# A fused group-norm, pair-mix and blur kernel on one core: wave 0 transposed as loaded, wave 1's statistics on ScalarE, filter and x1 statistics reordered

## What is computed

```python
def pair_mix(p, Wa, ba, Wb, bb, Wg, bg, Wo, bo):      # p (2, 64, 64, 64)
    a = p @ Wa + ba
    b = p @ Wb + bb
    g = sigmoid(p @ Wg + bg)
    ab = einsum('bijk,bikl->bijl', a, b)
    return g * ab @ Wo + bo

def gn(v): # 32 groups of 2 channels, each less its mean, over sqrt(variance + 1e-5)

x = x + pair_mix(gn(x), Wa, ba, Wb, bb, Wg, bg, Wo, bo)
x = x + depthwise_conv(gn(x), filt)   # 4x4 taps on a zero-stuffed map: 2x2 taps per output
```

## Time and profile before

| | us |
|---|---|
| median of 3 runs (lowest to highest) | 62.74 (62.19 to 62.99) |
| the profiled execution | 62.93 |
| its span | 61.0 |
| busy in the span: PE, DVE, POOL, ACT | 48.2, 41.5, 38.0, 29.3 |

### The profile page before, as it was taken

The page is one execution under the profiler, slowest core; times in us unless marked ns, Lnnn a source line. Parts: engine busy times, 40 slices in busy tenths (PEclk is TensorE's granted clock), DMA queues, the critical chain, the costliest instruction groups (busy, mean ns, idle before and its releaser), DMA issues.

```text
span 61.0 us, 2458 instructions
## 1 busy us (share of the span) xinstructions
PE 48.2 (79%) x1038; PEld 36.6 (60%) x1038; DVE 41.5 (68%) x111; ACT 29.3 (48%) x56; POOL 38.0 (62%) x51
## 2 busy tenths in 40 slices
PE   3999989998997985979999976998789899940000
PEld 3998878664865964756986735975468756400000
DVE  1073578888865679627479895479879978999200
ACT  5400005124494140784339999248892708990000
POOL 1000035809999599997281876984882997899500
PEclk9999999999999999999999999999999999999755
DMA  0899993000000000000000004031004004000494
GB/s 0 215 326 307 322 393 134 0 11 0 0 11 0 0 11 0 0 0 16 0 0 11 0 0 172 11 119 63 0 5 172 8 3 172 5 0 0 172 350 165
DMA packets 2604, 4.84 MB, mean 79 GB/s; under 512 B 289, under 2 KB 417, under 8 KB 2593
## 3 DMA queue, kind: packets, MB, share of 16 engines
q1 hardware_dynamic: 2592, 4.69, 22.4%
HBM read 2.59 MB, written 2.10 MB: 77 GB/s over the span
## 4 chain that ended last, share of the span: by engine, by line
PE 32%; POOL 24%; DVE 10%; issue 8%; ACT 4%; POOLq 2%; DVEq 0%
POOL y L253 11%; PE ps_ot L608 6%; PE ps_ab L641 6%; POOL rstd L218 6%; PE ps_ag L629 5%; POOL gn L240 5%; PE ps_ot L681 4%; PE ps_ag L653 2%; DVE y L468 2%; DVE bsb L445 2%; ACT gate L315 2%; PE ps_ab L665 2%; POOLq L55 2%; DVE part L414 2%; ACT rt L302 2%
## 5 line engine op out<-in xcount | busy, mean ns | idle before, releaser
L253 POOL TENSOR_TENSOR y<-y,prod 128x512 f32<-128x512 f32 x11 | 14.0, 1273 | 5.0 <-DVE y L468 4.6
L218 POOL TENSOR_TENSOR rstd<-veps,half 128x2 f32<-128x2 f32 (+1 forms) x7 | 5.7, 819 | 11.1 <-DVE veps L438 11.1
L583 PE MATMUL ps_ab<-zeros 128*128 128x128 f32 x54 | 9.3, 337 | 1.0 <-DVE zeros L486 1.0
L247 POOL TENSOR_TENSOR xb<-xs,par 128x512 f32<-128x512 f32 x8 | 8.5, 1098 | 1.6 <-issue 1.6
L583 PEld LDWEIGHTS ps_ab<-zeros 128*128 128x128 f32 x54 | 8.5, 244 | 1.0 <-DVE zeros L486 1.0
L315 ACT ACTIVATE gate<-ps_ag,par 128x512 f32<-128x512 f32 x8 | 5.5, 687 | 7.4 <-PE ps_ag L653 7.4
L302 ACT ACTIVATE rt<-ps_ot 128x512 f32<-128x512 f32 x7 | 4.0, 593 | 10.0 <-PE ps_ot L608 10.0
L345 ACT ACTIVATE prod<-x,coef 128x512 f32<-128x512 f32 x11 | 7.6, 711 | 0.0
L308 ACT ACTIVATE at<-ps_ag,par 128x512 f32<-128x512 f32 x8 | 5.5, 686 | 4.2 <-PE ps_ag L629 4.1
L454 DVE TENSOR_TENSOR zt<-ps_ab,gate 128x512 f32<-128x512 f32 x8 | 5.5, 684 | 2.8 <-ACT gate L315 2.3
L410 DVE BATCH_NORM_STATS2 part<-xs 128x6 f32<-128x512 f32 x8 | 5.4, 683 | 2.5 <-DMA xs<-x 2.5
(11 more groups left out here) (59 smaller groups left out, 71.4 us busy)
## 6 DMA issues: line engine op xcount, KB each, us to landing
xs<-x SPq DMA_DIRECT2D x8, 256.0 KB, 5.3
out<-y SPq DMA_DIRECT2D x8, 256.0 KB, 2.0
par<-params SPq DMA_DIRECT2D x1, 353.0 KB, 5.4
par<-params SPq DMA_DIRECT2D x1, 128.0 KB, 4.0
```

Of the source, the lines that this page charges most:

```text
L218: nc.gpsimd.tensor_tensor(job_of(rstd, job), job_of(veps, job), half[:, 0:columns(job)], ALU.pow).then_inc(rstd_done, 1)
L247: nc.gpsimd.tensor_tensor(xb[:, w, b, :, :], xs[:, w, b, :, :], bo.broadcast_to([128, ROWS, D]), ALU.add).then_inc(xb_ready, 1)
L253: return nc.gpsimd.tensor_tensor(y[:, w, b, :, :], y[:, w, b, :, :], prod[:, n % 2, k, :, :], ALU.add)
L583: nc.tensor.matmul(bank[:, 0:128], zeros[:], zeros[:], start=True, stop=True)
```

## The change

Wave 0 is not normalised and then transposed: TensorE transposes xs itself as soon as each image has landed (`raw_transposes`, image 0 in transpose mode and image 1 as a product with the identity, 64 columns each), into the same PSUM banks. `image_product` multiplies a broadcast column of means (later of roots) by columns of the averaging mask, so that the 16 values of the wave lie along the free axis of ps_f; VectorE subtracts the means while it copies out of PSUM (`centre`, four instructions of 128 x 256), and multiplies by the roots in place (`scaled_out`, four more), after which unit 0 and unit 1 can run. The masks are loaded in two pieces, the identity first. Ten, two, seven and four idle products become five, one and three.

Wave 1's statistics are made on ScalarE by four passes with a running sum (of x, then of squares of x less the mean), not by VectorE's reductions and the chain of small steps. The transposed halves of wave 0 are not copied by ScalarE.

The statistics of waves 2 and 3 and of each x1 move up by about a unit on VectorE and TensorE. The filter of wave w - 2 moves up on ScalarE, VectorE and GpSimd, and `add_bo(2)` moves back on GpSimd, behind the normalisations.

The diff, cut to its core:

```diff
             load(0, 0)
+            sp.dma_start(par[:, IDENT:MASKS], params[:, IDENT:MASKS]).then_inc(ident_in, 16)
             load(0, 1)
-            sp.dma_start(par[:, 0:MASKS], params[:, 0:MASKS]).then_inc(masks_in, 16)
+            sp.dma_start(par[:, 0:IDENT], params[:, 0:IDENT]).then_inc(masks_in, 16)
             for b in range(2):
                 load(1, b)
             sp.dma_start(par[:, MASKS:], params[:, MASKS:]).then_inc(params_in, 16)
...
-            add_bo(2)
             inverse_root(2)
             pool.wait_ge(rstd_done, 3)
             normalise(2)
             normalise(3)
+            add_bo(2)
             add_bo(3)
...
             add_products(0, 0)
-            add_products(0, 1)
             filter_coefs(1)
             filter_base(1)
+            add_products(0, 1)
             add_products(1, 0)
-            add_products(1, 1)
+            pool.wait_ge(right_ready, 4)
+            link(add_product(1, 1, 0))
             filter_coefs(2)
             filter_base(2)
+            add_product(1, 1, 1).then_inc(add_done, 1)
+            add_products(2, 0)
             filter_coefs(LAST)
-            add_products(2, 0)
             pool.wait_ge(right_ready, 6)
...
             def filter_base1(w):
                 act.wait_ge(coef_ready, w + 1)
+                act.wait_ge(halo_ready, w + 1)
...
-            transposed_out(0, 0)
+            for b in range(2):
+                act.wait_ge(xs_in[1][b], 16)
+                last = nc.scalar.activation(prod[:, 0, b, :, :], xs[:, 1, b, :, :], ACT.Copy, accum_out=sums[:, b:b + 1])
+            last.then_inc(sums_ready, 1)
+            act.wait_ge(stat_done, nth(1, 0))
+            nc.scalar.activation(nmu[:, 0, 1, :], ps_s[:, MEANS:MEANS + 2], ACT.Copy, scale=-1.0 / (ROWS * D)).then_inc(minus_ready, 1)
+            act.wait_ge(minus_ready, 2)
+            for b in range(2):
+                last = nc.scalar.activation(prod[:, 1, b, :, :], xs[:, 1, b, :, :], ACT.Square, bias=nmu[:, 0, 1, b:b + 1],
+                                            accum_out=squares[:, b:b + 1])
+            last.then_inc(squares_ready, 1)
...
                     if w >= 2:
+                        mean_column(w - 2)
                         halo_row(w - 2)
-                        mean_column(w - 2)
+                        filter_base1(w - 2)
+                        filter_product(w - 2, 0, 0)
                     gate_out(g)
                     if w >= 2:
-                        filter_product(w - 2, 0, 0)
+                        filter_product(w - 2, 0, 1)
                 else:
                     if 1 <= w < LAST:
                         transposed_out(w + 1, 0)
                     a_out(g)
                     if w >= 2:
-                        filter_product(w - 2, 0, 1)
+                        filter_product(w - 2, 1, 0)
                     if w == 0:
                         transposed_out(w + 1, 0)
                     if w < LAST:
                         transposed_out(w + 1, 1)
                     gate_out(g)
                     if w >= 2:
...
+            def centre(u, n):
+                dve.wait_ge(t_done, n + 1)
+                nc.vector.tensor_tensor(rows(u, n), by_image(ps_ot[:, n, :])[:, 8 * u:8 * u + 8].rearrange("p i r q -> p r i q"),
+                                        images(mu_image, u), ALU.subtract).then_inc(centred, 1)
+            def scaled_out(u, n):
+                dve.wait_ge(centred, 4)
+                return nc.vector.tensor_tensor(rows(u, n), rows(u, n), images(ps_f[:, 0:16], u), ALU.mult)
...
             deviation(0)
+            dve.wait_ge(images_done, 1)
+            nc.vector.tensor_copy(mu_image[:], ps_f[:, 16:32]).then_inc(mu_ready, 1)
+            dve.wait_ge(mu_ready, 1)
+            centre(0, 0)
             variance(0)
...
+            centre(0, 1)
+            centre(1, 0)
+            centre(1, 1)
+            dve.wait_ge(images_done, 2)
+            for u in range(2):
+                for n in range(2):
+                    last = scaled_out(u, n)
+                last.then_inc(rt0_ready, 1)
             x_part(2, 0)
...
                     aggregate(2)
+                    deviation(2)
+                    z_out(1)
+                    variance(2)
...
                 elif n == 0:
-                    job = 2 if g == 2 else X1JOB + w - 2
-                    deviation(job)
-                    variance(job)
                     b_out(g)
+                    if w >= 2:
+                        filter_right(w - 2, 0)
                     x1_out(w - 1, 0)
                     x1_out(w - 1, 1)
                     z_out(g)
-                    if w >= 2:
-                        filter_right(w - 2, 0)
+                    x1_part(w - 1, 0)
+                    if w == 1:
+                        x1_part(w - 1, 1)
+                        aggregate(X1JOB)
                 else:
-                    if w == 1:
-                        x1_part(w - 1, 0)
-                        x1_part(w - 1, 1)
                     b_out(g)
                     if w > 1:
-                        x1_part(w - 1, 0)
+                        x1_part(w - 1, 1)
+                        aggregate(X1JOB + w - 1)
+                    if w < LAST:
+                        deviation(X1JOB + w - 1)
+                    z_out(g)
                     if w == LAST:
-                        z_out(g)
-                    if w > 1:
-                        x1_part(w - 1, 1)
-                    aggregate(X1JOB + w - 1)
-                    if w < LAST:
-                        z_out(g)
-                    if w >= 2:
+                        filter_right(w - 2, 1)
+                        deviation(X1JOB + w - 1)
+                    else:
+                        variance(X1JOB + w - 1)
+                    if w == 2:
                         filter_right(w - 2, 1)
             job = X1JOB + LAST
             x1_out(LAST, 0)
-            deviation(job - 1)
             x1_out(LAST, 1)
             variance(job - 1)
...
+            def image_product(at, column):
+                for b in range(2):
+                    last = nc.tensor.matmul(
+                        ps_f[64 * b:64 * b + 64, at:at + 16], column[:, b:b + 1].broadcast_to([128, D]),
+                        average.rearrange("p (t u c q) -> p u c t q", t=2, u=2, q=8)[:, :, :, :, 0], start=True, stop=True)
+                last.then_inc(images_done, 1)
...
+            def raw_transposes(b, n):
+                pe.wait_ge(xs_in[0][b], 16)
+                for r in range(4):
+                    last = nc.tensor.matmul(columns_of(n, r)[64 * b:64 * b + 64], xs[:, 0, b, 4 * n + r, :], by_t,
+                                            start=True, stop=True, is_transpose=(b == 0))
+                if b == 1:
+                    last.then_inc(t_done, 1)
...
             pe.wait_ge(zeros_set, 1)
-            idle_products(10)
+            idle_products(5)
+            pe.wait_ge(ident_in, 16)
+            raw_transposes(0, 0)
+            raw_transposes(0, 1)
+            raw_transposes(1, 0)
             pe.wait_ge(masks_in, 16)
             stat_product(0, 0)
-            idle_products(2)
+            image_product(16, mv[:, 0, 0, :, 0])
+            raw_transposes(1, 1)
             stat_product(0, 1)
-            idle_products(7)
-            transposes(0, 0)
-            transposes(0, 1)
-            idle_products(4)
+            stat_product(1, 0)
+            idle_products(1)
+            pe.wait_ge(mu_ready, 1)
+            pe.wait_ge(rstd_done, 1)
+            image_product(0, rstd[:, 0, 0, :])
+            idle_products(3)
...
                 elif n == 0:
-                    job = 2 if g == 2 else X1JOB + w - 2
                     product_a(g)
-                    stat_product(job, 0)
-                    if w >= 2:
-                        halo(w - 2)
+                    if w == 2:
+                        halo(0)
+                    elif w == LAST:
+                        stat_product(X1JOB + 1, 1)
                     product_b(g)
-                    stat_product(job, 1)
+                    if w == LAST:
+                        halo(1)
...
                 product_g(g)
+                if g == 1:
+                    stat_product(2, 0)
+                elif g == 3:
+                    stat_product(X1JOB, 0)
                 product_ab(g)
-            idle_products(2, ps_ot[:, 0, :])
+                if g == 1:
+                    stat_product(2, 1)
+                elif g == 3:
+                    stat_product(X1JOB, 1)
+                elif n == 1:
+                    stat_product(X1JOB + w - 1, 0)
+            idle_products(1, ps_ot[:, 0, :])
             product_o(LAST)
-            stat_product(X1JOB + LAST - 1, 0)
+            stat_product(X1JOB + LAST - 1, 1)
...
```

114 lines of the change are left out of this document (59 added, 55 removed).

## The result

| | before | after |
|---|---|---|
| median, us (lowest to highest) | 62.69 (62.19 to 62.99) | 64.95 (64.22 to 66.51) |
| profiled execution; its span | 62.93; 61.0 | 65.26; 63.4 |
| busy PE, DVE, POOL, ACT | 48.2, 41.5, 38.0, 29.3 | 49.2, 42.9, 37.8, 32.6 |

The change makes the kernel slower: ratio 1.029, 95% interval 1.016 to 1.041. The forecast was 63.2 in a range of 61.3 to 64.9. The median lies 0.05 above that range; the ratio times 62.74 is 64.5, inside it. The sign of the difference was right. Its size was not: 0.5 forecast, 1.8 by the ratio, 2.3 by the medians.

The account below looks back on a forecast made before the run. Two relays bound the kernel: TensorE with helpers in the first two thirds, GpSimd in the last quarter, ending it. Product a +0.1 and the rest +0.4 gave span 61.5, 63.4 profiled, median 63.2; range 61.3 to 64.9.

Parts of the forecast that it names:

- The head: Program start up to unit 0's product a: a at 11.3 us where it was 11.19, bounds 10.1 and 12.9.
- a before 10.7: Sign that the forecast is wrong: unit 0's product a, expected at 11.0 to 11.6, comes before 10.7.
- the squares' product: TensorE in the head: expected at 8.3, halfway between 7.7 (clock up) and 9.0 (down); it was 6.78.
- The multiplications: VectorE in the head, by the roots: 0.35 to the next and 0.42 for the last, 1.38 for four.
- The gain of 1.48: Root of waves 2 and 3 on GpSimd starts at a + 8.24 against a + 9.72, so 1.48 sooner.
- The block on GpSimd, and unit 4: GpSimd's queue grows to 9.8, unit 4 waits for its coefficients: z of unit 4 (z4) at a + 22.2, was 21.04.
- Rival 2: Faster: the filter does not hold unit 4, so the 1.48 mostly stays; 61.4 us, chance 0.22.
- From z4 to z7: From z of unit 4 to z of unit 7: same distance as before, 12.3 to 12.4.
- The tail: From the variance of wave 2's x1, GpSimd needs 8.75 and ends at a + 46.45, against a + 46.06 before.
- Wrong if the end is VectorE's: Sign that the forecast is wrong: VectorE ends the program, instead of GpSimd's last addition at 57.5 to 58.
- Rival 1: Slower: TensorE stays at 1.2 GHz in the head, squares' product later than 8.9; 64.4 us, chance 0.27.
- Rival 3: Wave 1's sums on ScalarE come late and hold the root's image on TensorE: a at 11.9, 63.8 us, chance 0.11.

Follow-up runs that it names:

- experiment 12: Kernel of 6 plus an unread one-input GpSimd operation on SBUF beside the right taps of waves 1 and 2: 62.87 us, one execution.
- experiment 4: Changed kernel with add_bo(2) put back ahead of the root of waves 2 and 3 on GpSimd: 63.43 us, ratio 1.015 against the kernel before.
- experiment 1: The changed kernel run again unaltered: 66.32 us, ratio 1.060 against the kernel before.
- Experiment 5: Changed kernel with GpSimd's additions held until VectorE's right tap of the same stage is done: 63.54 us, ratio 1.012 against the kernel before.
- 6: Changed kernel with add_bo(2) early and GpSimd's additions held behind the right taps: 61.62 us, ratio 0.981 against the kernel before.
- experiment 10: Body of 6 with the head of the kernel before (normalise, then transpose; wave 1 on VectorE): 62.02 us, ratio 0.993 against the kernel before.
- 9: Kernel of 6 run again in five rounds: 62.13 us over 14 runs, ratio 0.987 against the kernel before; its profiled execution took 63.81.
- 8: Changed kernel with nine idle TensorE products ahead of wave 3's transposes, to fill the gap: 65.59 us, ratio 1.027 against the kernel before.
- 3: The changed kernel's new order of the body with the head of the kernel before: 65.60 us, ratio 1.036 against the kernel before.

## Why the prediction was right, and where it failed

**The head: a at 11.3, forecast range 10.1 to 12.9.** Measured 10.22 in the profile after, and 10.22 to 12.26 in the eleven profiled executions with this head, with 11.01 in the middle; the old head gave 10.66 to 11.19 in three. The range was right. The forecast's own sign of being wrong, a before 10.7, did appear in the profile after. The width comes mostly from the speed of TensorE's pieces: the second half of x was in use at 4.49 in after and at 4.52 in experiment 12, but the sixteen raw pieces took 2.36 in the one and 3.25 in the other, and a was at 10.22 and 11.20; with the second half at 5.63 (experiment 4), a was at 11.01. Within the sum, the squares' product was expected at 8.3 and came at 7.39. Both terms ahead of it were too large: the averaging mask landed at 4.9, 2.8 behind its issue at 2.10 (6.1 to 6.9 was forecast, from the landing of a 128 KB load), so the means' product at 5.94 waited for the raw pieces alone. The multiplications took 1.41 for four, as forecast (1.38). The Trainium skill's estimate of 0.42 for 256 elements ("VectorE: DVE Perf Modes", section on the trn2 errata) agrees with the traces, where one of the subtractions, with one of its inputs in PSUM, takes 0.42.

**The gain of 1.48 at the root of waves 2 and 3.** Right: a + 8.23 against a + 8.24.

**The block on GpSimd, and unit 4.** Right, each step to 0.2: root a + 17.93 (18.05), tap a + 20.14 (20.25), gate a + 20.60 (20.75), z4 a + 22.01 (22.2). That the block is the cause was an argument then; experiment 4 shows it. Rival 2 (the filter doesn't hold unit 4) is refuted.

**From z4 to z7 "the same distance as before (12.3 to 12.4)".** This step failed: 14.25. Two costs were in it, and neither had a term.

- *The clock behind TensorE's gap.* The forecast said that the transposes of wave 3 wait for x1, and priced what is late by the queue alone. In after, 1 and 5 a gap of 2.07, 1.88 and 2.47 us was followed by the lower level and 5.2 from z4 to z5, instead of 3.96. I had looked for the lower clock in the head and not where my own working made the gap. The page's granted clock of before showed 9 in all of the middle, but there TensorE never had such a gap.
- *The right tap beside GpSimd.* The change moves `add_products(0, 1)` ahead of the wait for the tap, and splits the one for wave 1 in the same way. I read this as GpSimd's order and never asked what runs beside what. In the kernel before each addition waited for the tap that was just running, which kept the two apart. Experiment 5 prices it: 0.9 at unit 6, and in the tail 0.55 for GpSimd's end (1.0 for VectorE's).

**The tail: GpSimd's end at a + 46.45 ends the program.** That GpSimd's end sets the program's was right: the last stores are issued right behind it, as before. Its time failed, mostly as a consequence: a + 49.36. The tail's own sum was also too small. From the variance of wave 2's x1 to GpSimd's end 8.75 was forecast, the pieces alone with next to nothing for waits; it took 9.92, of which 1.49 were waits (0.63, 0.26 and 0.60), and 9.35 in experiments 5 and 6, where the taps are short. "Wrong if the end is VectorE's" came true of the engines and not of the stores: VectorE's last instruction ends at a + 50.06, and in 6 and 10, without the missed costs, it is still 0.31 behind GpSimd's. One reason stands in the traces and is tested by no run: the change puts ScalarE's halo row of the last wave behind `filter_base1`, and VectorE waits 0.63 for it in the tail of 5, 6 and after, where the kernel before has no such wait. That is about the whole of 12.84 against 12.26.

**The sum.** The forecast span was 61.5, the profiled one 63.4. In the terms of GpSimd's end: head −1.1 against the forecast, clock +1.2, taps +1.4, the rest +0.3, together 1.8. With a at 11.3 the same body would have ended yet 1.1 later, and experiment 1 shows an execution nearer to that (a at 10.97, 65.97 us). So the number 63.2 was nearer to the measurement than its working was, and by luck: an early head covered over a third of what lay behind it.

**The rivals.** Rival 1, TensorE at 1.2 GHz in the head, had the right time (64.4) by the wrong place; it happens in some executions (9, with the squares' product at 9.04, past its mark of 8.9, and a at 12.26; in 8 that product was at 8.68, and three idle products, 1.65 instead of 0.94, held a until 12.08). The Trainium skill's rule beside it ("TensorE: Matmul & The Clock Gate", PE-mode transpose) that the higher level does not engage for transposes does not hold here: four transposes take 0.63 in experiment 4, and about 1.1 only while TensorE is at the lower level behind the gap (after, 1 and 5). Rival 3, wave 1's sums late, did not occur: they were done at 7.8, before the root.

What stays open: why a gap lowers the clock in after, 1 and 5 (2.07, 1.88 and 2.47 us) and not in 3 (2.59 us). No run separates the gap from what TensorE did ahead of it. Open too is what the moved body does apart from the two costs: with the clock up and the taps short (experiment 10 against before) z4 to z5 is 0.38 longer and z5 to z6 0.76 shorter.

## What to carry to other kernels

When a statistic is made sooner, look at the queue of the engine that uses it: here the gain of 1.5 us lay behind a step of 2.15 that the same change had moved into that queue, and moving this one step back gave 2.9 us back (1.3 of it by TensorE's clock). A wait may be worth its time for what it keeps apart: before removing one between VectorE and GpSimd, list the instructions that will then run side by side, and look whether VectorE's has two inputs in SBUF. And every delay that a forecast finds for TensorE is a gap on TensorE; price the stage behind it at both clock levels. And the engine whose instruction ends last need not be what the last store waits for: read the start of the last stores.

## What the runs showed of the hardware that I had not expected

- A VectorE operation with two SBUF inputs (128x512, fp32, 0.75 us alone) that starts 0.07 behind a GpSimd operation on SBUF ends 0.55 behind GpSimd's end: 1.75 us beside an addition of 1.27, 1.09 beside a one-input operation of 0.62. With one input in PSUM it takes 0.74 to 0.76 beside the same additions. GpSimd pays too when an addition follows the waiting tap at once: four additions took 5.54 to 5.55 instead of 5.21 to 5.23 (in after, 1.60 for the second of the four, 1.27 to 1.29 for its neighbours).
- The granted clock at the same place of the same program differs from execution to execution. In three profiles it fell behind a gap of TensorE (2.07, 1.88, 2.47 us), and in a fourth, with 2.59, it did not; each fall cost 1.2 to 1.3 us in the unit behind it.
- With transposes near the start of the program TensorE's speed there varies from execution to execution: the same sixteen pieces in 2.36 to 3.81 us, a between 10.22 and 12.26, where the head with more idle products gave 10.66 to 11.19.
- A ScalarE pass with a running sum brings a second instruction of 0.19 (ACTIVATION_READ_ACCUMULATOR) behind it, hidden here.
